# Two instructions moved in the softmax pipeline of a latent-attention kernel: one exponential on ScalarE, one column sum on TensorE

## The reference

```python
q_hk = (hidden_q @ Wq.T).reshape(b, s, H, K)
q_big = jnp.einsum('bshk,hkq->bshq', q_hk, w_kc_q)      # layer 0 applies rope to it
q_r = jnp.einsum('bshq,hqr->bhsr', q_big, W_qr)
k_r = jnp.einsum('bld,hdr->bhlr', kv_rope, W_kr)
scores = jnp.einsum('bhsr,bhlr->bhsl', q_r, k_r)
attn = jax.nn.softmax(scores, axis=-1)
ctx_c = jnp.einsum('bhsl,bld->bhsd', attn, kv_rope)
ctx_lat = jnp.einsum('bhsd,hkd->bshk', ctx_c, w_kc_kv)
out = ctx_lat.reshape(b, s, H * K) @ Wo.T
```

## Time and profile before

| | |
|---|---|
| three runs, median (lowest to highest) | 3631.51 us (3626.7 to 3635.6) |
| the profiled execution's own time | 3626.7 us |
| its span, first to last instruction | 3625.0 us |
| TensorE, VectorE, ScalarE, GpSimd busy | 96%, 45%, 24%, 22% |
| mean granted TensorE clock | 0.985 |
| instructions | 42943 |
| chain that ended last, by engine | PE 82%, DMA 9%, DVE 4%, ACT 3% |

### The profile page before, as it was taken

One profiled execution on the slowest core, in us unless ns is written; L12 is line 12 of the kernel. 1 busy time (PEld: TensorE's weight loads), 2 busy tenths in 40 slices (PEclk: granted clock), 3 DMA queues, 4 the chain that ended last, 5 costly groups with the idle time before them and its releaser, 6 DMA issues.

```text
span 3625.0 us, 42943 instructions
## 1 busy us (share of the span) xinstructions
PE 3466.3 (96%) x16460; PEld 1809.5 (50%) x16461; DVE 1647.0 (45%) x1958; ACT 862.9 (24%) x1254; POOL 790.8 (22%) x745
## 2 busy tenths in 40 slices
PE   7799999999999878999999989999999999999999
PEld 4365565456456433333333346556465564554554
DVE  7764565466456451111111135536355265662661
ACT  1131032022023211111111125325144252220110
POOL 5600410320130011222222210000000002780760
PEclk9999999999999989999999989999999999999999
DMA  5631132122113286998888974536255152340320
GB/s 180 201 121 46 66 98 62 53 92 72 49 47 101 90 325 199 324 355 308 297 310 295 363 235 147 145 112 179 93 156 169 63 162 67 124 154 1 139 104 37
DMA packets 93028, 556.63 MB, mean 154 GB/s; under 512 B 11288, under 2 KB 11424, under 8 KB 74976
## 3 DMA queue, kind: packets, MB, share of 16 engines
q1 hardware_dynamic: 58288, 445.28, 34.2%
q0 software_dynamic: 31392, 93.76, 9.8%
q10 hardware_dynamic: 3216, 15.68, 1.4%
HBM read 517.62 MB, written 40.71 MB: 154 GB/s over the span
## 4 chain that ended last, share of the span: by engine, by line
PE 82%; DMA 9%; DVE 4%; ACT 3%; issue 1%; SPq 1%; POOL 0%; POOLq 0%; DVEq 0%; ACTq 0%
PE PS L917 14%; PE PS L2155 10%; PE PS L1066 9%; PE PS L1836 9%; PE PS L880 8%; DMA bias<-in_b 6%; PE PS L2169 5%; PE PS L1860 5%; PE PS L777 4%; PE PS L902 3%; PE PS L794 3%; PE PS L861 2%; PE PS L1003 2%; PE PS L809 2%; ACT Sb L1177 1%
## 5 line engine op out<-in xcount | busy, mean ns | idle before, releaser
L917 PE MATMUL PS<-Sb,kvN 121*128 121x400 f32 (+1 forms) x1536 | 537.1, 500 | 1.9 <-ACT Sb L1164 1.9
L1836 PE MATMUL PS<-W,hT 128*64 128x512 f32 x2208 | 505.7, 600 | 18.4 <-DMA bias<-in_b 15.1
L917 PEld LDWEIGHTS PS<-Sb,kvN 121*128 121x128 f32 (+1 forms) x1536 | 286.7, 190 | 208.4 <-ACT Sb L1164 2.8
L1409 POOL TENSOR_TENSOR qrope<-qrope,rt 128x400 f32<-128x400 f32 x192 | 209.5, 1113 | 742.8 <-DVE rt L1282 742.8
L2155 PE MATMUL PS<-xh,wq 128*128 128x400 f16 x2048 | 346.8, 332 | 0.9 <-DVE xh L1244 0.9
L880 PE MATMUL PS<-kvT,wkr 128*128 128x363 f32 x1024 | 345.4, 480 | 1.0 <-ACT KR L1093 1.0
L1929 DVE TENSOR_TENSOR gu<-PS,bias 128x512 f32<-128x512 f32 x69 | 47.7, 692 | 640.0 <-PE PS L1836 640.0
L1066 PE MATMUL PS<-wb,ctxl 128*128 128x512 f32 x768 | 331.7, 593 | 4.2 <-ACT ctxl L1093 4.2
L2111 POOL TENSOR_SCALAR gtq<-stg,thr 128x1024 f16<-128x1024 f32 x96 | 288.3, 3019 | 181.6 <-DMA stg<-in_F 130.4
L1836 PEld LDWEIGHTS PS<-W,hT 128*64 128x64 f32 x2208 | 153.4, 138 | 309.6 <-issue 287.5
L2155 PEld LDWEIGHTS PS<-xh,wq 128*128 128x128 f16 x2048 | 200.3, 98 | 147.2 <-DVE xh L1244 1.2
(11 more groups left out here) (284 smaller groups left out, 3800.1 us busy)
## 6 DMA issues: line engine op xcount, KB each, us to landing
W<-in_W SPq DMA_DIRECT2D x96, 2048.0 KB, 12.2
stg<-in_F SPq DMA_DIRECT2D x32, 1536.0 KB, 6.4
kvT<-kvT_d SPq DMA_DIRECT2D x64, 726.0 KB, 4.1
kvN<-kvN_d SPq DMA_DIRECT2D x64, 726.0 KB
absin<-in_F POOLq DMA_DIRECT2D x48, 512.0 KB, 4.5
hn<-in_F POOLq DMA_DIRECT2D x48, 512.0 KB, 4.8
wb<-in_WB SPq DMA_DIRECT2D x8, 2560.0 KB, 8.8
wc_h<-in_WC SPq DMA_DIRECT2D x32, 576.0 KB, 5.6
```

Of the source, the lines that this page charges most:

```text
L917: mm = nc.tensor.matmul(PS[:, value_bank(b) + dc, 0:GW], kvN[b % 2][0:k, lc, dc * P:(dc + 1) * P], Sb[b % 2][0:k, lc, :], start=lc == 0, s ...
L1409: ins = nc.gpsimd.tensor_tensor(qrope[k % NR][:, i, :], qrope[k % NR][:, i, :], rt[k % 2][:, 1 - i, :], ALU.add)
L1836: mm = nc.tensor.matmul(PS[g * BS:(g + 1) * BS, 2 + u % 2, :], hT2[k][:, c, half * BS:(half + 1) * BS], W2[:, q, o:o + N1], start=c == 0, ...
```

## The change

Two edits, both only of order. On TensorE, in stage 7, `softmax_sum` of batch element 6 moves from ahead of the block of the following work to behind it. On ScalarE, `exponential(0)` used to be put off to stage 1, behind the copies of that stage's scores; now it stands at the end of stage 0, as the exponentials of all other stages stand at the end of theirs.

```diff
--- before.py
+++ after.py
@@ -1024,7 +1024,6 @@
                         values(hg, st - 1, 1)
 
                 scores(hg, B - 1)
-                softmax_sum(hg, B - 2)
                 if not more:
                     lift(0)
                 elif ly == 0:
@@ -1033,6 +1032,7 @@
                 else:
                     pe.wait_ge(sem(f"{p}_se"), n_ev * (hg + 1))
                     fold_m(hg + 1, 0)
+                softmax_sum(hg, B - 2)
                 largest(B - 1)
                 values(hg, B - 2, 0)
                 if more and ly == 1:
@@ -1179,8 +1179,6 @@
                             nc.scalar.activation(to[:, 0], src[:, 0], ACT.Copy).then_inc(sem(f"{p}_se"), 1)
                             nc.scalar.activation(to[:, 1], src[:, 1], ACT.Identity, bias=cst[0:LP, C_PAD:C_PAD + 1]).then_inc(sem(f"{p}_se"), 1)
                     early, late = keys_of(ly, st)
-                    if st == 1:
-                        exponential(0)
                     if early:
                         c_key(hg, *early)
                     elif not more:
@@ -1195,8 +1193,7 @@
                             fold(hg + 1, 0, n)
                     if late:
                         c_key(hg, *late)
-                    if st >= 1:
-                        exponential(st)
+                    exponential(st)
                     if ly == 1:
                         absolute(hg, 3 * st + 2)
                     if ly == 0 and st == 2:
```

## The result

The changed kernel takes 3663.98 us (median of 4 runs, 3660.64 to 3666.15); the kernel before 3629.11 us (median of 4). The ratio is 1.0086, 95% interval 1.0073 to 1.0099: 31 us slower, and by the medians 35. The forecast was 3659 us and 28 us slower.

A forecast was written before the change was run, and what follows sets the result against it. TensorE, busy for 96% of the span, was taken to bound the kernel. The terms 11.6 + 7.3 + 3.2 + 6 made 28 us slower, 3659 us on the median of 3631.5, range 3643 to 3674.

The forecast's parts named there:

- The stall of layer 0: Stage 1, head groups 1 to 4: TensorE's scores wait for ScalarE's first copy behind the exponential, 3.2 us a group.
- The stall of layer 1: Stage 1, head groups 5 to 8: TensorE's present wait grows from 2.4 to 4.4 us, 2.0 us added a group.
- What comes back: Stage 1, groups 1 and 5: TensorE's waits for the exponential before the values go, 1.9 us together; table load hidden.
- Edit 2: TensorE, stage 7: softmax sum of batch element 6 behind the following matmuls, 0.4 or 0.5 us a group, 3.2 in all.
- The clock: TensorE's clock falls from 2.4 to 1.2 GHz behind the stage 1 stalls, 1.8 us a fall: 6 us added together.
- clock falls everywhere, and for long: Rival: TensorE's clock falls after all eight stage 1 stalls, 22 + 17.4 = 39.5 us slower, 3671 us; chance 16%.
- The rival of an absorbed stall: Later TensorE idle time between stages 2 and 7 absorbs the stage 1 stall, leaving about 3 us: 3635; chance 7%.

The follow-up runs named there:

- edit 2 alone: Kernel before, with only the softmax sum of batch element 6 moved behind the following matmuls on TensorE in stage 7: 3630.87 us, ratio 1.0004.

## Why the prediction was right

The mechanism was the one forecast, and the forecast of 28 us is near the 31 to 35 that were measured. Term by term, some of that is luck, as errors of both signs are in the sum.

- The stall of layer 0: worked out as 3.2 us; TensorE stood still for 3.3 in each of four groups, and the third part of the scores starts 3.2 us later in the stage than before. The step from the shift's end to the exponential (0.04) was 0.03, its length 2.10 was 2.11.
- The stall of layer 1: 4.34 us in each group, forecast 4.4, in place of 1.95, 2.36, 2.32 and 2.49.
- What comes back: TensorE's waits for the first exponential went, and the table load cost nothing, as forecast. In group 5 the profile before has 0.7 us for this wait because slow matmuls covered a part of it; with the clock held by dummy matmuls it was 1.3.
- The stalls in sum, without the clock: 11.2 us in layer 0 and 6.4 in layer 1, together 17.6, by the two kernels with dummy matmuls. The forecast was 11.6 + 7.3 = 18.9, over by 1.3.
- Edit 2: 3.7 by the trace, forecast 3.2. The block behind was 0.1 us a group longer than the 5.37 I took. Group 4 was 0, as forecast.
- The clock was the mis-sized term: forecast 6 us, measured 10.4. The falls cost 189.1 - 174.2 = 14.9 us in the changed kernel and 161.2 - 156.7 = 4.5 before, each less the same kernel with its stalls filled. (Executions differ: with the second profile of the changed kernel, or that of edit 2 alone for the kernel before, the difference is 8.7 to 13.7, over the 6 in every pairing.) The price of 1.8 a fall was right: eight falls at 1.3 to 2.7 are 1.9 on average. One fall more came than I took (eight, not seven). Above all, the three falls before had not cost the 6.6 that I counted as paid already, but 0.6 in group 5, 2.5 in group 7 and 1.4 in group 8: a mean clock times the length of a window also counts slow time in which TensorE was waiting anyway. The case "clock falls everywhere, and for long" came true in its first half alone.
- Outside the sum: 4.2 us in the profile, in parts of the program that the change does not touch. The forecast had no term for it. At the two ends of the program it is scatter; whether the 3.3 us of the experts' phase belong to the change is open.
- The sum: 1.3 over in the stalls, 0.5 under in edit 2, 4.4 under in the clock and 4.2 outside make the 7.8 us between 28.1 and the 35.9 of the profile.
- The rival of an absorbed stall had its deciding point right: between the scores of stage 2 and those of stage 7 there is next to no idle time, and the scores of stage 7 come later by just what those of stage 2 do.

The Trainium skill ("TensorE: Matmul & The Clock Gate", "HAM oscillation — how this bites in real kernels") has it that a kernel which waits some 3 to 5 us for DMA in every step runs the matmuls behind each wait slow. That a gap is paid a second time in this way held at eight stalls of eight in the changed kernel, at three of four shorter ones before and at two of four in the profile of edit 2 alone, but not at the waits of 3.21 and 3.02 us that the exponential between the copies made.

## What to carry to other kernels

An engine that is busy for a quarter of the time can still bound a kernel at one place: look at what stands ahead of the instruction that the busiest engine waits for, and put there only what that engine needs next. Here the copies of the scores were needed at once. The exponential was needed only by the values, which TensorE began 6.3 us after the scores of the stage (478.48 in the earlier trace rows), just after it ended at 484.62. From the timeline of head group 2 before:

```profile
484.78 4.30 PE L917 MATMUL PS<-Sb,kvN 121*128 121x400 f32 x12
```

The same question asked about the kernel before found the wait of an unrelated sum for its DMA at the same place, worth 12 us.

## What the runs showed of the hardware

- In the profile after, a stall of TensorE of 3.3 us cost 4.5 on the path in head groups 2 and 3, as the clock was then at 1.2 GHz over a part of the matmuls behind it, and 5.9 in group 4; one of 4.3 us cost 5.9 to 6.3 (head groups 6 to 8). Stalls of 2.0 to 2.6 us sometimes did this and sometimes not. The waits of 1.1 us (stage 7) never did, and with the exponential between the copies neither did those of 1.7 and 1.8 us nor those of 3.0 and 3.2.
- Filling a stall with matmuls whose result nobody reads made the program 17 us faster, though no instruction on the path starts earlier by it than the wait allows.
- Shortening a stall from 4.34 to 3.31 us brought next to nothing in stage 1 of layer 1 in the one profile there is, as the slow stretch then covered more of the matmuls.
